# A vision tower's last layer norm and expert MLP: one pass in pairs of groups, rewritten as a five-step pipeline that starts inside the last attention

## The reference, cut to what matters

```
h = tok(x)
h = h + linear_attention(layernorm(h))
h = h + moe(layernorm(h))
h = h + l1_attention(layernorm(h))
h = h + route_mlp(layernorm(h))        # the part that is changed

def route_mlp(x):                       # x: 128 images x 64 tokens x 64
    y = relu(x @ Wi.T + bi)             # 64 -> 128
    for l in range(2):                  # e = route_id of the token's pair
        y = relu(y @ Ws[l].T + bs[l] + y @ Wr[l, e].T + br[l, e] + y)
    return y @ Wo.T + bo                # 128 -> 64
```

## Time and profile before

| what | us |
| --- | --- |
| median of 3 runs (lowest, highest) | 2650.24 (2647.89, 2652.99) |
| profiled execution, its own time | 2650.77 |
| its span, from first to last instruction | 2648.9 |
| TensorE busy | 2259.4 (85%) |
| VectorE busy | 2253.5 (85%) |
| GpSimd busy | 1754.7 (66%) |
| ScalarE busy | 1474.8 (56%) |

### The profile page before, as it was taken

How to read it: one execution, slowest core, us unless ns; L and a number is a source line. 1 busy time by engine, 2 the same in 40 slices (tenths; PEclk the granted TensorE clock), 3 DMA queues, 4 the chain that set the end, 5 groups by cost and what they waited for, 6 DMA issues and landing times.

```text
span 2648.9 us, 45720 instructions
## 1 busy us (share of the span) xinstructions
PE 2259.4 (85%) x12251; PEld 971.9 (37%) x12251; DVE 2253.5 (85%) x2718; ACT 1474.8 (56%) x3767; POOL 1754.7 (66%) x1015
## 2 busy tenths in 40 slices
PE   5649999999388989899898989989898998989366
PEld 3433333333133333333333333333333333333255
DVE  2877778777699999999999999999999999999532
ACT  0325555555166666666666666666666666666234
POOL 0112333333188888889888888888888888888311
PEclk8879999999599999999999999999999999999678
DMA  5200000000022221222212122221212222121000
GB/s 130 61 0 1 1 0 0 0 0 0 19 50 51 50 50 45 51 50 51 50 47 52 46 50 50 50 50 47 52 46 50 50 51 50 47 52 46 13 12 20
DMA packets 163209, 101.97 MB, mean 38 GB/s; under 512 B 55773, under 2 KB 161182, under 8 KB 163039
## 3 DMA queue, kind: packets, MB, share of 16 engines
q1 hardware_dynamic: 162858, 101.41, 15.5%
q10 hardware_dynamic: 316, 0.12, 0.0%
HBM read 10.63 MB, written 4.19 MB: 6 GB/s over the span
## 4 chain that ended last, share of the span: by engine, by line
PE 62%; DVE 23%; issue 10%; DVEq 2%; ACT 1%; DMA 1%; POOL 1%; ACTq 0%; SPq 0%; POOLq 0%
DVE score L1364 17%; PE pp L760 16%; PE pp L754 7%; PE pp L594 5%; PE pp L725 3%; PE pp L615 2%; PE pp L681 2%; PE pp L673 2%; PE pp L619 2%; PE pp L689 2%; PE pp L669 2%; PE pp L679 2%; PE pp L616 2%; PE pp L620 2%; PE pp L586 2%
## 5 line engine op out<-in xcount | busy, mean ns | idle before, releaser
L1364 DVE TENSOR_REDUCE score<-pp 128x16 f32<-128x1024 f32 x1408 | 1647.1, 1219 | 103.2 <-PE pp L760 83.6
L1473 POOL TENSOR_TENSOR absd<-absd 128x2560 f32<-128x2560 f32 (+4 forms) x640 | 1453.8, 2272 | 199.8 <-ACT absd L1004 159.5
L760 PE MATMUL pp<-blocks,pick 128*128 128x512 f16 x2816 | 817.3, 383 | 154.9 <-DVE score L1364 150.5
L1004 ACT ACTIVATE absd<-pp 128x512 f32<-128x512 f32 x1280 | 695.5, 598 | 369.4 <-PE pp L754 365.5
L760 PEld LDWEIGHTS pp<-blocks,pick 128*128 128x128 f16 x2816 | 211.3, 98 | 590.6 <-DVE score L1364 421.3
L754 PE MATMUL pp<-blocks,pick 128*128 128x512 f16 x1280 | 400.3, 383 | 2.1
L1449 POOL TENSOR_TENSOR absd<-absd,yw 128x512 f32<-128x512 f32 x112 | 142.1, 1269 | 319.0 <-DVE yw L1286 319.0
L938 ACT ACTIVATE absd<-pp 128x512 f32<-128x512 f32 x256 | 150.8, 596 | 148.2 <-PE pp L616 146.9
L1302 DVE SCALAR_TENSOR_TENSOR absd<-pp,absd 128x512 f32<-128x512 f32 x256 | 172.6, 688 | 53.1 <-ACT absd L938 38.4
L754 PEld LDWEIGHTS pp<-blocks,pick 128*128 128x128 f16 x1280 | 119.9, 98 | 248.6 <-ACT absd L1004 84.2
L986 ACT CAST qk<-pp 128x512 f16<-128x512 f32 x130 | 76.0, 585 | 191.2 <-PE pp L682 191.2
(11 more groups left out here) (209 smaller groups left out, 2578.7 us busy)
## 6 DMA issues: line engine op xcount, KB each, us to landing
blocks<-qk SPq DMA_DIRECT2D x1032, 64.0 KB, 2.0
attn<-score SPq DMA_DIRECT2D x1024, 16.0 KB, 1.8
xs<-xn SPq DMA_DIRECT2D x66, 32.0 KB, 1.8
big<-in_wrb_t SPq DMA_DIRECT2D x1, 2064.0 KB
big<-in_x_rows SPq DMA_DIRECT2D x4, 512.0 KB, 6.4
token_rows<-big SPq DMA_DIRECT2D x8, 256.0 KB, 2.0
big<-in_L_ffn_w SPq DMA_DIRECT2D x4, 512.0 KB, 9.8
out<-big SPq DMA_DIRECT2D x16, 128.0 KB, 2.0
```

Source lines behind the costliest of these rows:

```text
L760: mm = pe.matmul(ps[bank + n], pick[:, unit % 8 + n, :], blocks[:, b, unit // 16, unit // 8 % 2, :], start=True, stop=True)
L1004: nc.scalar.activation(absd[odd][:, 16 * u + 8 * n:16 * u + 8 * n + 8, :], ps[4 + n].rearrange("p (h w) -> p h w", w=D), ACT.Abs).then_inc ...
L1364: dve.tensor_reduce(score[:, odd, b, 16 * d:16 * d + 16], pp[:, bank:bank + 2, :].rearrange("p n (h w) -> p (n h) w", w=D), AX.X, ALU.add, ...
L1473: nc.gpsimd.tensor_tensor(x[:, :, 0:w], x[:, :, 0:w], x[:, :, w:2 * w], ALU.add).then_inc(X["tree"], 1)
```

## The change

- The last layer norm is done in quarters of 16 pairs (`layernorm_part`), each cut into four pieces between which VectorE does other work. The first quarter and its pieces lie between the last operations of the attention.
- The MLP is unrolled. In step i TensorE does turn(i), first(i-1), layer 1 of i-2, layer 2 of i-3 and out(i-4); the other engines follow the same order, and three weight buffers rotate. The last pair's attention products, turn and fan-in lie in steps 0 to 2.
- Of a group's four weight choices GpSimd does three and VectorE one, each as one copy of both layers (258 columns) after one register load. The copy of xn is gone: the turns read xn. The add of bo is done in h, 16 pairs at a time, on GpSimd, and the result is added in h and sent from there.
- The sums Ws + I and Wr + Ws move from VectorE behind the last layer norm to GpSimd ahead of its `hx` add, that is, beside the layer norm ahead of the L1 attention.
- The last image's five `absd` tiles are reduced by VectorE in one instruction instead of GpSimd's tree. `xT5` has its own buffer, and its padding is set at the very start.

```diff
+        xT5 = sb("xT5", [KA, 2, 512])
+        squares = absd0[:, 0:1024].rearrange("p (n d) -> p n d", d=D)
+        wsel = [t.rearrange("p (l j n) -> p l j n", l=2, j=4) for t in (big3[:, 0:1032], big3[:, 1032:2064], absd0[:, 1024:2056])]
...
+        def layernorm_part(dve, c):
+            step, n = ln_step[3], 11 * c
...
+            dve.wait_ge(X["sum"], size * c + size)
+            dve.tensor_reduce(total, h[:, at, :], AX.X, ALU.add).then_inc(step, 1)
...
+            dve.tensor_scalar(mean, total, 1.0 / D, None, ALU.mult).then_inc(step, 1)
...
+            dve.tensor_tensor(x, h[:, at, :], mean.unsqueeze(2).to_broadcast(wide), ALU.subtract).then_inc(step, 1)
+            yield
...
+            dve.tensor_tensor(squares, x, x, ALU.mult).then_inc(step, 1)
...
+            dve.tensor_reduce(total, squares, AX.X, ALU.add).then_inc(step, 1)
...
+            dve.tensor_scalar(var, total, 1.0 / D, EPS, ALU.mult, ALU.add).then_inc(step, 1)
+            yield
+            dve.wait_ge(ln_sd[3], c + 1)
+            dve.reciprocal(r, sd).then_inc(step, 1)
...
+            yield
+            dve.wait_ge(step, n + 11)
+            dve.tensor_tensor(x, x, r.unsqueeze(2).to_broadcast(wide), ALU.mult).then_inc(xn_ready[3], 1)
+            yield
+
+        def select_weights(eng, g, js, done):
+            if g >= 3:
+                eng.wait_ge(M["h2"], 4 * (g - 2))
+            for j in js:
+                r = eng.value_load(route[0:1, 4 * g + j:4 * g + j + 1], min_val=0, max_val=EXPERTS - 1)
+                op = eng.tensor_copy(wsel[g % 3][:, :, j, :].unsqueeze(2), wc[:, :, bass.ds(r, 1), :])
+            op.then_inc(M[done], 1)
@@ TensorE @@
+            def mlp_turn(g):
+                pe.wait_ge(xn_ready[3], g // PARTS + 1)
+                if g:
+                    pe.wait_ge(M["xT"], g)
...
+            def mlp_layer(g, l):
+                pe.wait_ge(M[f"h{l}"], (1, 4)[l] * (g + 1))
+                pe.wait_ge(M["selp"], g + 1)
+                pe.wait_ge(M["seld"], g + 1)
+                if g:
+                    pe.wait_ge(M[f"h{l + 1}"], 4 * g)
...
+            last_turn(last - 1)
+            last_attend(last - 1, 0)
+            turn_y(last - 1)
+            fan_in(last - 1)
+            last_turn(last)
             pe.wait_ge(mlp_in, MLP_IN)
+            for i in range(G4 + 4):
+                if i < G4:
+                    mlp_turn(i)
+                if 1 <= i < G4 + 1:
+                    mlp_first(i - 1)
+                if 2 <= i < G4 + 2:
+                    mlp_layer(i - 2, 0)
+                if 3 <= i < G4 + 3:
+                    mlp_layer(i - 3, 1)
+                if i >= 4:
+                    mlp_out(i - 4)
+                if i == 0:
+                    last_attend(last, 1)
+                if i == 1:
+                    turn_y(last)
+                if i == 2:
+                    fan_in(last)
@@ ScalarE @@
+            def root(c):
+                act.wait_ge(ln_step[3], 11 * c + 6)
...
+            exponentials(last, 0, False)
+            exponentials(last, 1, False)
+            root(0)
+            turned_attn(last)
+            for i in range(G4 + 3):
+                if i % 4 == 2 and i // 4 + 1 < PARTS:
+                    root(i // 4 + 1)
...
@@ VectorE @@
             reciprocals(last - 1)
             finish(last - 2, slice(last - 2, last - 1))
+            dve.wait_ge(X["pooled"], 2 * last + 1)
+            dve.wait_ge(X["abs"], 2 * NA * (2 * last + 2))
+            dve.tensor_reduce(score[:, 1, 1, 16 * ND:256], absd[1], AX.X, ALU.add).then_inc(X["pooled"], 1)
...
+            norm = layernorm_part(dve, 0)
+            next(norm)
             gated(last - 1)
+            next(norm)
+            select_weights(dve, 0, (3,), "seld")
+            reciprocals(last)
+            next(norm)
             finish(last - 1, slice(last - 1, last))
+            next(norm)
+            select_weights(dve, 1, (3,), "seld")
             gated(last)
+            for i in range(G4 + 4):
+                if 3 <= i < G4 + 1:
+                    select_weights(dve, i - 1, (3,), "seld")
+                if i >= 4:
+                    add_output(i - 4)
+                if i < 4 * (PARTS - 1):
+                    if i % 4 == 0:
+                        norm = layernorm_part(dve, i // 4 + 1)
+                    next(norm)
+                if i == 1:
+                    finish(last, slice(last, last + 1))
@@ GpSimd, ahead of the hx add @@
+            pool.wait_ge(mlp_in, MLP_IN)
+            pool.wait_ge(l1_in, L1_IN)
+            for l in range(2):
+                nc.gpsimd.tensor_tensor(ws[:, l, 0:HID], ws[:, l, 0:HID], ident[:], ALU.add).then_inc(wc_ready, 1)
+            pool.wait_ge(wc_ready, 2)
+            for l in range(2):
+                nc.gpsimd.tensor_tensor(wc[:, l], wc[:, l], ws[:, l, :].unsqueeze(1).to_broadcast([P, EXPERTS, HID + 1]),
+                                        ALU.add).then_inc(wc_ready, 1)
             pool.wait_ge(xn_ready[2], 1)
@@ GpSimd, end @@
-            batch(2 * last + 1, last, 1, 1, 4)
             normalise(last - 1, False)
...
+            pool.wait_ge(wc_ready, 4)
+            select_weights(pool, 0, (0, 1, 2), "selp")
+            output_bias(0)
             normalise(last, False)
+            for g in range(1, G4):
+                select_weights(pool, g, (0, 1, 2), "selp")
+                if g % 4 == 2 and g // 4 + 1 < PARTS:
+                    output_bias(g // 4 + 1)
```

More of the change, by code:

```diff
@@ L272, in build @@
         M = {n: sem("e_" + n) for n in (
-            "xs", "xT_ps", "xT", "h0_ps", "h0", "sel0", "sel1", "h1_ps", "h1", "h2_ps", "h2", "o_ps", "hb", "fin", "out", "free", "sent")}
+            "xT_ps", "xT", "h0_ps", "h0", "selp", "seld", "h1_ps", "h1", "h2_ps", "h2", "o_ps", "hb", "fin", "out")}
         block = ctx.enter_context(nc.Block())
@@ L424, in _ @@
             sp.wait_ge(X["xs"], 16 * (PAIRS + 2))
[L426 to L433, removed]
+            for g in range(G4):
+                sp.wait_ge(M["fin"], g + 1)
+                sp.dma_start(out.rearrange("(p b) s d -> (b s) p d", b=2)[:, 4 * g:4 * g + 4, :],
+                             h[:, 4 * g:4 * g + 4, :]).then_inc(M["out"], 16)
             sp.wait_ge(M["out"], 16 * G4)
@@ L810, in _, with last_turn @@
             fan_in(last - 2)
-            for p, odd in ((last - 1, 0), (last, 1)):
+            def last_turn(p):
                 pe.wait_ge(X["attk"], p + 1)
@@ L820, in _ @@
                     attend_part(p, odd, part)
-                turn_y(p)
-                fan_in(p)
-            pe.wait_ge(mlp_in, MLP_IN)
[L826 to L855, removed]
@@ new lines, in mlp_turn, with mlp_first @@
+            def mlp_turn(g):
+                pe.wait_ge(xn_ready[3], g // PARTS + 1)
+                if g:
+                    pe.wait_ge(M["xT"], g)
+                for j in range(4):
+                    m = 1 if j else 2
+                    mm = pe.transpose(ps[0][0:D * m, P * j:P * j + P],
+                                      xn[:, 4 * g + j:4 * g + j + m, :].rearrange("p n d -> p (n d)"), ident[:])
+                mm.then_inc(M["xT_ps"], 1)
+            def mlp_first(g):
+                pe.wait_ge(M["xT"], g + 1)
+                if g:
+                    pe.wait_ge(M["h0"], g)
+                pe.matmul(ps[1], wi[:], xT5[:, g % 2, :], start=True, stop=True).then_inc(M["h0_ps"], 1)
@@ new lines, in mlp_layer @@
+            def mlp_layer(g, l):
+                pe.wait_ge(M[f"h{l}"], (1, 4)[l] * (g + 1))
+                pe.wait_ge(M["selp"], g + 1)
+                pe.wait_ge(M["seld"], g + 1)
+                if g:
+                    pe.wait_ge(M[f"h{l + 1}"], 4 * g)
+                for j in range(4):
+                    mm = pe.matmul(ps[2 + l][:, P * j:P * j + P], wsel[g % 3][:, l, j, 0:HID],
+                                   hm[:, l, g % 2, P * j:P * j + P], start=True, stop=True)
+                mm.then_inc(M[f"h{l + 1}_ps"], 1)
@@ new lines, in mlp_out @@
+            def mlp_out(g):
+                pe.wait_ge(M["h2"], 4 * (g + 1))
+                if g:
+                    pe.wait_ge(M["fin"], g)
+                for j in range(4):
+                    mm = pe.matmul(ps[4][:, D * j:D * j + D], hm[:, 2, g % 2, P * j:P * j + P], wo[:], start=True, stop=True)
+                mm.then_inc(M["o_ps"], 1)
+            last_turn(last - 1)
[3 more added lines that the diff above has]
+            last_turn(last)
@@ L1081, in _ @@
             values_f(last, 1)
[L1082 to L1104, removed]
+            def root(c):
+                act.wait_ge(ln_step[3], 11 * c + 6)
+                at = slice(PAIRS // PARTS * c, PAIRS // PARTS * (c + 1))
+                nc.scalar.activation(stat[:, 3, at], stat[:, 2, at], ACT.Sqrt).then_inc(ln_sd[3], 1)
@@ new lines, in mlp_turned, with mlp_first, mlp_layer @@
+            def mlp_turned(g):
+                act.wait_ge(M["xT_ps"], g + 1)
```

(23 more changed lines are left out.)

66 lines of the change are left out of this document (47 added, 19 removed).

## The result

The median falls from 2649.56 us to 2578.14 us (4 runs each, 2576.05 to 2578.80 after). The measured ratio is 0.9724, interval 0.9710 to 0.9739 (these two medians alone give 0.9730). The forecast of 2590 was 12 us too high, and its range, which began at 2579, missed the time by 1. The sign and the mechanism held; a size did not.

The account below looks back on a forecast made before the run. The L1 attention fills TensorE and VectorE; the tail is a chain of short operations with no engine full, which pipelining shortens to TensorE's pace. 2650.8 - 64.1 (tail) + 3.5 (sums) = 2590.2, stated as 2590, range 2579 to 2611.

Parts of the forecast that it names:

- sums on GpSimd ahead of the h add: Before the L1 attention: GpSimd's sums hold up VectorE's layer norm pass L287, +3.5 us, bounds 0 and 8.2.
- reduce to exponentials: Attention's drain: VectorE's reduce ends 2.7 us before GpSimd's tree did, so the exponentials come at 2478.9 instead of 2481.54.
- turn 0 to turn 4: Pipeline start, 2485.5 to about 2504: steps 0 to 2 at the low clock, step 3 warm.
- waits and low clock in them: Steps 8 and 12 wait for a quarter's last pass behind an add: 1.8 us each, 3.6 in all.
- steps 16 to 19: Pipeline's end: 4, 3, 2 and 1 batches plus ScalarE's latency, 11.6 us.
- the price of a full step: MLP steps 4 to 15: TensorE's five batches take 5.2 us a step, bounds 4.6 and 5.5; 62.4 for twelve.
- in GpSimd's slack: Bias add in h, 2.2 us a quarter on GpSimd, fits beside its choices and costs nothing.
- the two table loads: ScalarE at the pipeline's start: two more loads, to tanh and back, run ahead of waits and cost nothing.
- (b): Rival, MLP steps: GpSimd paces, 13 groups at 6.0 us, total 2601; chance 0.17.
- (c): Rival, MLP steps: TensorE's clock stays low, all steps +37 to 2627, half +18 to 2608; chance 0.17.
- (d): Rival: slower than before, since each GpSimd choice waits for VectorE, 3.3 us a choice, 9.8 a group; chance 0.03.
- (a): The forecast itself: TensorE paces at 4.6 to 5.5 us a step, total 2583 to 2600; chance 0.63.

Follow-up runs that it names:

- c4: Changed kernel with all four quarters of the norm done one after the other behind the attention's end, the pipeline after them; 2598.21 us, ratio 0.9799.
- d3: Changed kernel with the edits of c1, d1 and d2 together; 2563.16 us, ratio 0.9663.
- c2: Changed kernel with GpSimd's bo add to quarters 1 to 3 one group of choices later; 2573.44 us.
- c7: Changed kernel with the last image's score tiles added by GpSimd's tree again, without the VectorE reduce; 2584.03 us.
- d2: Changed kernel with the first piece of quarter 1 ahead of the last pair's gate on VectorE; 2574.17 us.
- c1: Changed kernel with the sums Ws + I and Wr + Ws behind GpSimd's h add instead of ahead of it; 2575.73 us, ratio 0.9720.
- c0: The changed kernel measured once more, unaltered, as the zero for other runs; 2579.38 us, ratio 0.9728.
- d1: Changed kernel with VectorE's last pass of a quarter ahead of the add of the step before; 2570.74 us.

## Why the prediction was wrong in its size

All figures are from the changed kernel's profile. To take out how early the attention ends, the terms but the first count from the last pair of score reduces, at 2461.92 before and 2464.59 after.

| term | predicted | measured |
| --- | --- | --- |
| sums on GpSimd ahead of the h add | +3.5 | +3.0 |
| reduce to exponentials | 17.0 | 15.5 |
| reduce to turn 0 | 23.6 | 22.2 |
| turn 0 to turn 4 | 18.5 | 17.0 |
| twelve full steps without waits | 62.4 | 47.2 |
| waits and low clock in them | 3.6 | 9.8 |
| steps 16 to 19 | 11.6 | 10.7 |
| reduce to TensorE's end (the sum without the first two rows) | 119.7 | 106.8 |

**The step that failed is the price of a full step**: "Sum 4.90. Modelled ends overlap the next start a little; against that each of the five batches has waits of its own, which I put at 0.3 in all. A full step is 5.2 us, bounds 4.6 ... and 5.5". It is 3.92 to 4.09 in nine of the twelve steps, 3.93 in c4's twelve and in most of d3's. I added durations of batches, which overlap: in the steps above each batch starts 0.16 ahead of the modelled end of the one before it, so the five durations sum to 4.74 where the starts give 3.93. The trace before had what was needed: eight L845 took 1.13 and one of them 0.28, so they are 0.12 from start to start. By (duration less one instruction) / (n - 1) x n, the five rows give 0.47, 0.9, 0.97, 0.97 and 0.94, 4.3. And of the waits I added, none shows in an undisturbed step. This term alone was 15.2 too high, more than the whole error of 12.

**What hid part of it**: the stalls, 9.8 in place of 3.6. The two waits at turns 8 and 12 were placed right, and the first measured as forecast, 1.77 for 1.8. The second was 3.78, because GpSimd's bo add met the pass (the bias was costed "in GpSimd's slack", which was true for GpSimd and not for VectorE; 2.1 by c2), and 2.8 more went to a step at the low clock. Most of the rest is 0.55 in each of the steps 7 and 11, in which ScalarE starts late by the root. Fast steps and long stalls partly cancelled, so that the miss of 12 is smaller by luck: with the step at 3.93 and all else as forecast, the sum would have been 2590.2 - 15.2 = 2575.0.

**The start**: most of the 1.5 by which the exponentials came sooner than forecast is the queue shown at c7. Turn 0 to turn 4 is near the forecast for another reason than mine. I costed steps 0 to 2 at the low clock and saw no wait. In this profile TensorE was at full speed from 2490 on (turn 0.66, Wi 1.02), then stood 3.09 before turn 3, since ScalarE's copy stood behind the root, and the root behind quarter 1's sums; only behind this wait was the clock low again. The "nothing" for the two table loads that "run ahead of waits" was right, but what was queued behind the root itself was not counted. d2 shows the wait to be one of order.

**The rivals.** (b), GpSimd as the pace: where nothing meets it, a choice costs 0.40 for the copy and 0.27 for the gap ahead of it, 2.0 a group in place of the 3.3 taken, far under the pace. (c), a low clock throughout: it was 0.95. Its mechanism was there in steps 0, 3 and 12. (d) never came near.

**The range** took its low end from a step of 4.6 (12 x 0.6 under the forecast, 2583) and 4 for the drain. That bound does not follow from its own words, since a tenth off each of five batches makes 4.4; and the truth, 3.93, lay under both. So no chance stood where the truth lay. Two more sums are off: with the lock's bound of 0, (a) itself reaches down to 2579.5, and the terms given for steps 0 to 3 add up to 17.7, not to 18.5.

What held of the price paid was the block of VectorE by GpSimd's sums, drawn from two rows of the kernel before; c1 shows its 3.0, and moving the line gives back at least 2.5. The reason given for leaving the reduce L283 out of the block, "since L283 has one input", was not one: L1337 in the earlier trace rows has one input and took 8.30, until GpSimd's add ended, and L285, which was held here, has one too. That the reduce kept its 4.42 was right all the same.

## What to carry to other kernels

Price a batch on TensorE by the distance of starts, or by (duration less one instruction) / (n - 1) x n. The sum of the durations of these short batches was a fifth too high (4.74 against 3.93), and that becomes the whole error once the engine is full. In a pipeline written out by hand, look in each engine's queue for the one operation that a whole step waits for (here a layer norm's last pass behind an add that must wait anyway, and a copy behind a root), and put it ahead. An operation moved to GpSimd "into its slack" can still take its price from VectorE: 3.0 at L285 and 2.1 at L346 here.

## What the runs showed of the hardware that was not expected

- A VectorE scaling of 64 numbers (L285) was held 3.0 us by a GpSimd add, though it has one input; the reduce of 4096 beside it was not held at all.
- TensorE's granted clock after a short wait is not fixed by the wait: behind 1.77 us the step took 3.98 in the changed kernel and 5.61 in c0, in the same place of the same program. Over the seven profiles with 1.77 or 1.78 before turn 8, two had the low clock behind it. Behind 0.34 us (d1, d3) it never fell, behind 3.78 us before turn 12 it always did (six profiles).
- Kernels with the same attention code reached its end up to 8 us apart (last score reduces between 2461.2 and 2468.9 over the thirteen profiles from the change on). Up to 3.5 of this is there before the L1 attention begins (L283 starts between 666.7 and 670.1). From there to the last score reduces ten of the eleven profiles with the sums ahead of the h add took 1798.6 to 1799.0, the changed kernel's own 1797.4, and the two with the sums moved 1794.5 and 1794.7. That is more than the 2.5 that their operations show; why is open.
